# A mixture-of-experts kernel on one core: two blocks sorted together in the last step, running sums in reduced-precision products, and a new table of slots

## What is computed

```python
x = x + 0.5 * ffn0(layernorm(x))   # step 0
x = x + attn0(layernorm(x))
x = x + 0.5 * ffn0(layernorm(x))   # step 1
x = x + 0.5 * ffn1(layernorm(x))   # step 2
x = x + attn1(layernorm(x))
x = x + 0.5 * ffn1(layernorm(x))   # step 3
```

```python
kv = cumsum(einsum('bhtf,bhtg->bhtfg', K, V), axis=2)
Z = 1.0 / (einsum('bhtf,bhtf->bht', Q, cumsum(K, axis=2)) + 1e-06)
out = einsum('bhtf,bhtfg->bhtg', Q, kv) * Z[..., None]
```

## Time and profile before

| | us |
|---|---|
| median of 3 runs | 795.04 |
| lowest, highest | 790.27, 796.32 |
| the profiled execution, its own time | 787.4 |
| its span, first to last instruction | 785.7 |
| mean granted clock of TensorE, share of full speed | 0.929 |

### The profile page before, as it was taken

How to read it: one execution, slowest core, us unless ns; L and a number is a source line. 1 busy time by engine, 2 the same in 40 slices (tenths; PEclk the granted TensorE clock), 3 DMA queues, 4 the chain that set the end, 5 groups by cost and what they waited for, 6 DMA issues and landing times.

```text
span 785.7 us, 15361 instructions
## 1 busy us (share of the span) xinstructions
PE 631.2 (80%) x4586; PEld 571.3 (73%) x4586; DVE 392.2 (50%) x1357; ACT 255.5 (33%) x531; POOL 315.9 (40%) x352
## 2 busy tenths in 40 slices
PE   1298577969979796777888795999898988988975
PEld 1298466949768596677788794888787777887975
DVE  4373432725437163524354351775674855754165
ACT  1143332533415242323333241423423434232320
POOL 3545351271442516270716235225335354154314
PEclk9999897999999899887999798998999999989989
DMA  9378482735628266565767574665464554756942
GB/s 313 118 227 243 129 251 85 207 119 152 188 70 232 89 181 195 162 185 157 231 179 230 149 211 128 178 166 142 144 172 134 172 140 122 221 140 177 297 131 44
DMA packets 113796, 133.83 MB, mean 170 GB/s; under 512 B 10947, under 2 KB 76755, under 8 KB 113334
## 3 DMA queue, kind: packets, MB, share of 16 engines
q1 hardware_dynamic: 105526, 116.06, 51.0%
q0 software_dynamic: 8192, 16.79, 7.3%
HBM read 104.09 MB, written 28.71 MB: 169 GB/s over the span
## 4 chain that ended last, share of the span: by engine, by line
PE 58%; issue 19%; DVE 7%; another core or an unknown queue 5%; POOL 5%; ACT 4%; DMA 1%; SPq 1%; POOLq 0%; DVEq 0%; ACTq 0%
PE up_gate L983 16%; PE up_gate L976 13%; PE y L937 9%; PE side L991 3%; PE side L1057 2%; PE y L939 2%; PE side L1007 2%; PE side L1002 1%; POOL rows_dram L477 1%; DVE hidden L661 1%; ACT hidden L562 1%; PE side L1091 1%; POOL b_rstd L469 1%; PE side L1065 1%
## 5 line engine op out<-in xcount | busy, mean ns | idle before, releaser
L661 DVE TENSOR_TENSOR hidden<-up_gate,hidden 128x256 f32<-128x256 f32 (+1 forms) x240 | 116.0, 488 | 250.9 <-ACT hidden L562 84.0
L983 PE MATMUL up_gate<-rows_T,up 128*128 128x128 f32 x1440 | 199.2, 288 | 43.5 <-issue 21.7
L983 PEld LDWEIGHTS up_gate<-rows_T,up 128*128 128x128 f32 x1440 | 184.1, 202 | 57.0 <-issue 35.7
L562 ACT ACTIVATE hidden<-up_gate 128x256 f32<-128x256 f32 (+1 forms) x240 | 104.6, 436 | 322.4 <-PE up_gate L976 123.8
L477 POOL DMA_INDIRECT rows_dram<-rms_out,rows_of x128 | 128.2, 1002 | 176.9 <-DVE rows_of L801 142.4
L976 PE MATMUL up_gate<-rows_T,up 128*128 128x128 f32 x960 | 142.0, 295 | 18.4 <-ACT rows_T L567 6.6
L976 PEld LDWEIGHTS up_gate<-rows_T,up 128*128 128x128 f32 x960 | 128.5, 207 | 27.2 <-DVE hidden L661 13.2
L495 POOL DMA_INDIRECT y_rows<-y_dram,rows_of x120 | 122.1, 1018 | 56.6 <-issue 36.0
L937 PE MATMUL y<-down,hidden 128*128 x480 | 77.0, 285 | 4.8 <-issue 2.5
L937 PE MATMUL y<-down_a,hidden 128*128 x480 | 76.8, 285 | 0.0
L937 PEld LDWEIGHTS y<-down,hidden 128*128 128x128 f32 x480 | 66.6, 201 | 5.8 <-issue 5.8
(11 more groups left out here) (172 smaller groups left out, 671.8 us busy)
## 6 DMA issues: line engine op xcount, KB each, us to landing
up<-in_up SPq DMA_DIRECT2D x120, 352.0 KB
up<-in_up SPq DMA_DIRECT2D x120, 256.0 KB
rows<-rows_dram SPq DMA_DIRECT2D x48, 256.0 KB
y_dram<-y_tile SPq DMA_DIRECT2D x45, 256.0 KB
rows_dram<-zeros SPq DMA_DIRECT2D x12, 256.0 KB, 4.2
rows<-rows_dram SPq DMA_DIRECT2D x16, 192.0 KB
y_dram<-y_tile SPq DMA_DIRECT2D x15, 192.0 KB
rows_dram<-rms_out,rows_of POOLq DMA_INDIRECT x128
```

The costliest lines, as they stand in the source:

```text
L562: act.activation(hid[n % 4][:, 0:w], src, ACT.Silu).then_inc(silu_done, 1)
L661: dve.tensor_tensor(h, u, h, ALU.mult).then_inc(mult_done, 1)
L983: last = pe.matmul(U[q % 3][:, c * P:(c + 1) * P], upW[n % RING][:, at + c * P:at + (c + 1) * P], rows_, start=True, stop=True)
```

## The change

Group 4 = blocks 1 and 2 is new, and used in step 3 alone: 15 + 23 + 15 = 53 tiles there, so 233 slots in all. Block 1 still has 45 slots from its end to the group's start, block 2 has 30 and block 3 has 38. Block 2 therefore takes its own offsets (WAY = 1): attention 7 to 18, routing from 18, assign at 20, and scatter from 21, which now writes all 16 pieces of the group in the slots 186 to 193. The group's rows are loaded at slot 190 and transposed at 193, and its first tile is slot 195. LAG puts block 2's gathering 7 slots behind block 1's. Attention of the other blocks goes from offsets 14 to 31 to 8 to 22, with the following routing 9 slots earlier.

Each running-sum product becomes two: ACT copies k times v to fp32r (`kv_hi`), DVE subtracts that from the original (`kv_lo`), and PE multiplies both by fp32r ones. All other slots move too, among them LATE_MATRIX and the early store of the last group.

```diff
-GROUPS = [[0], [1], [2], [3]]
-STEP = [[0, 1, 2, 3], [0, 1, 2, 3], [0, 1, 2, 3], [0, 1, 2, 3]]
+GROUPS = [[0], [1], [2], [3], [1, 2]]
+STEP = [[0, 1, 2, 3], [0, 1, 2, 3], [0, 1, 2, 3], [0, 4, 3]]
...
-LAG = (1, 13, 9, 17, 9)
-
-COMBINE = (((8, 11),),
-           ((10, 13),),
-           ((7, 8),),
-           ((7, 9),))
-ATTENTION = (({3: 12, 4: 12, 5: 12, 6: 13, 7: 15, 8: 16, 9: 17, 10: 17, 11: 17, 12: 18, 13: 18, 14: 18, 15: 19},),
+LAG = (1, 24, 19, 32, 7)
+
+COMBINE = (((8, 10),),
+           ((8, 11),),
+           ((6, 6), (6, 6),),
+           ((7, 10),))
+ATTENTION = (({3: 11, 4: 11, 5: 11, 6: 12, 7: 14, 8: 15, 9: 16, 10: 17, 11: 18, 12: 19, 13: 19, 14: 19, 15: 20},),
              None,
-             ({3: 14, 4: 15, 5: 15, 6: 17, 7: 18, 8: 21, 9: 21, 10: 21, 11: 23, 12: 23, 13: 24, 14: 24, 15: 25, 16: 26, 17: 28, 18: 28, 19: 28, 20: 30, 21: 31},),
+             ({3: 8, 4: 8, 5: 8, 6: 8, 7: 10, 8: 11, 9: 11, 10: 11, 11: 12, 12: 12, 13: 15, 14: 15, 15: 16, 16: 17, 17: 18, 18: 19, 19: 19, 20: 21, 21: 22},
+              {3: 7, 4: 7, 5: 8, 6: 8, 7: 9, 8: 10, 9: 10, 10: 10, 11: 12, 12: 12, 13: 14, 14: 14, 15: 14, 16: 15, 17: 16, 18: 16, 19: 17, 20: 18, 21: 18},),
              None)
...
-         ({"stats": 31, "guess": 31, "root": 31, "norm": 31, "skip": 33, "z": 33, "score": 33, "first": 33, "second": 33, "rank": 35, "assign": 35, "weights": 36, "scatter": 37},))
-WAY = ((0, 0, 0, 0), (0, 0, 0, 0), (0, 0, 0, 0), (0, 0, 0, 0), (0, 0, 0, 0))
+         ({"stats": 22, "guess": 22, "root": 22, "norm": 22, "skip": 29, "z": 24, "score": 24, "first": 24, "second": 24, "rank": 26, "assign": 26, "weights": 27, "scatter": 28},
+          {"stats": 18, "guess": 18, "root": 18, "norm": 18, "skip": 24, "z": 19, "score": 19, "first": 19, "second": 19, "rank": 20, "assign": 20, "weights": 26, "scatter": 21},))
+WAY = ((0, 0, 0, 0), (0, 0, 0, 0), (0, 0, 0, 0), (0, 0, 1, 0), (0, 0, 0, 0))
...
-LATE_T, LATE_STORE, LATE_LOAD = (LATE_AT - LATE + at for at in (-7, 3, 5))
-LATE_MATRIX = [LATE_AT - LATE + at for at in (8, 9, 10, 11, 12, 13, 15)]
+LATE_T, LATE_STORE, LATE_LOAD = (LATE_AT - LATE + at for at in (-10, -9, -7))
+LATE_MATRIX = [LATE_AT - LATE + at for at in (-5, 2, 5, 6, 8, 9, 12)]
...
-                    if END_ROUND[r] + (STORE if (s, g) != LAST else 3) - 1 == t:
+                    if END_ROUND[r] + (STORE if (s, g) != LAST else 1) - 1 == t:
...
+                    if j in (13, 14, 15, 16):
+                        t = j - 13
+                        act.wait_ge(kv_ready, 4 * ka - 3 + t)
+                        act.activation(kv_hi[t][:, :], R[3 + t], ACT.Copy).then_inc(hi_ready, 1)
...
+                if l == 1 and j in (14, 15, 16, 17):
+                    t = j - 14
+                    dve.wait_ge(hi_ready, 4 * ka - 3 + t)
+                    dve.tensor_tensor(kv_lo[t][:, :], R[3 + t], kv_hi[t][:, :].bitcast(F32), ALU.subtract).then_inc(lo_ready, 1)
...
-                        pe.wait_ge(kv_ready, 4 * ka - 3 + t)
+                        pe.wait_ge(lo_ready, 4 * ka - 3 + t)
...
-                        last = pe.matmul(o, tri[:, :], R[3 + t], start=True, stop=(t % 2 == 0))
+                        pe.matmul(o, tri_r[:, :], kv_hi[t][:, :], start=True, stop=False)
+                        last = pe.matmul(o, tri_r[:, :], kv_lo[t][:, :], start=False, stop=(t % 2 == 0))
                         if t % 2:
-                            last = pe.matmul(o, ones[:, :], R[2 + t], start=False, stop=True)
+                            pe.matmul(o, ones_r[:, :], kv_hi[t - 1][:, :], start=False, stop=False)
+                            last = pe.matmul(o, ones_r[:, :], kv_lo[t - 1][:, :], start=False, stop=True)
```

More of the change, by code:

```diff
@@ L77 @@
              None)
-ROUTE = (({"stats": 2, "guess": 2, "root": 2, "norm": 3, "skip": 9, "z": 5, "score": 6, "first": 8, "second": 8, "rank": 10, "assign": 10, "weights": 11, "scatter": 16},),
-         ({"stats": 19, "guess": 19, "root": 20, "norm": 21, "skip": 23, "z": 23, "score": 24, "first": 25, "second": 27, "rank": 29, "assign": 29, "weights": 38, "scatter": 29},),
-         ({"stats": 15, "guess": 15, "root": 16, "norm": 20, "skip": 29, "z": 22, "score": 23, "first": 24, "second": 25, "rank": 27, "assign": 27, "weights": 36, "scatter": 29},),
-         ({"stats": 31, "guess": 31, "root": 31, "norm": 31, "skip": 33, "z": 33, "score": 33, "first": 33, "second": 33, "rank": 35, "assign": 35, "weights": 36, "scatter": 37},))
@@ L82 @@
-WAY = ((0, 0, 0, 0), (0, 0, 0, 0), (0, 0, 0, 0), (0, 0, 0, 0), (0, 0, 0, 0))
+ROUTE = (({"stats": 2, "guess": 2, "root": 2, "norm": 3, "skip": 10, "z": 4, "score": 6, "first": 7, "second": 7, "rank": 8, "assign": 8, "weights": 10, "scatter": 16},),
+         ({"stats": 20, "guess": 22, "root": 23, "norm": 23, "skip": 23, "z": 26, "score": 27, "first": 28, "second": 28, "rank": 30, "assign": 30, "weights": 30, "scatter": 30},),
+         ({"stats": 11, "guess": 12, "root": 14, "norm": 14, "skip": 16, "z": 15, "score": 16, "first": 16, "second": 17, "rank": 19, "assign": 19, "weights": 24, "scatter": 29},),
+         ({"stats": 22, "guess": 22, "root": 22, "norm": 22, "skip": 29, "z": 24, "score": 24, "first": 24, "second": 24, "rank": 26, "assign": 26, "weights": 27, "scatter": 28},
+          {"stats": 18, "guess": 18, "root": 18, "norm": 18, "skip": 24, "z": 19, "score": 19, "first": 19, "second": 19, "rank": 20, "assign": 20, "weights": 26, "scatter": 21},))
@@ L193, in macaron @@
         xT = sb("attn_xT", NT)
+        kv_hi = [sb(f"kv_hi{i}", NT, F32R) for i in range(TB)]
+        kv_lo = [sb(f"kv_lo{i}", NT, F32R) for i in range(TB)]
+        tri_r = sb("tri_r", P, F32R)
+        ones_r = sb("ones_r", P, F32R)
         spare = sb("spare", 2)
@@ L312, in macaron @@
         qkv_ready, min_ready, v_ready, exp_ready = sem("qkv_ready"), sem("min_ready"), sem("v_ready"), sem("exp_ready")
-        phi_ready, kv_ready, kcum_ready, den_used = sem("phi_ready"), sem("kv_ready"), sem("kcum_ready"), sem("den_used")
+        phi_ready, kv_ready, hi_ready, lo_ready, kcum_ready, den_used = sem("phi_ready"), sem("kv_ready"), sem("hi_ready"), sem("lo_ready"), sem("kcum_ready"), sem("den_used")
         cum_ready, cum_used = sem("cum_ready"), sem("cum_used")
@@ L641, in _ @@
             act.activation(spare[:, 0:1], ones[:, 0:1], ACT.Silu)
+            act.activation(tri_r[:, :], tri[:, :], ACT.Copy)
+            act.activation(ones_r[:, :], ones[:, :], ACT.Copy).then_inc(const_pe, 1)
             act.wait_ge(norm_loaded, 32)
@@ L1144, in _ @@
             pe.wait_ge(consts, 7)
-            pe.wait_ge(const_pe, 1)
+            pe.wait_ge(const_pe, 2)
             pe.wait_ge(norm_loaded, 32)
```

## The result

The changed kernel takes **819.11 us** (median of 4 runs, 816.34 to 828.08), the kernel before on the same chip 795.68 (790.27 to 799.23): the ratio is **1.032**, 95% interval 1.022 to 1.042. I had forecast 777.3. It is slower, and the range to 797 doesn't hold it.

What follows compares the result with a forecast made beforehand. PE was taken to set the pace, with stalls between. The terms -14.9 - 8.0 + 4.0 - 3.4 + 7.0 - 3.0 + 0.6 sum to -17.7 us, giving 777.3 on the median's base; whole range 757 to 797.

Steps and rivals of the forecast that it cites:

- The moved slots of layer 0 keep their number of operations and of bursts; I count 0.: Layer 0's moved slots: no change in time, with 4 us to either side of 337 us.
- "-8.0" for the sums: Running sums on PE: twelve one-pass fp32r products replace six fp32 ones a block, saving 8.0 us over four blocks.
- What the sums need in return, +4.0: ACT's copies and DVE's subtractions for the sums: ACT hides its part, DVE's costs 1 us a block, +4.0 us.
- Earlier attention, -3.4: Layer 1's attention: the sum of k moves to three slots behind phi, so its waits go, -3.4 us.
- The common group, +7.0: Blocks 2 and 3 before the group's tiles: waits for scattered rows, late normalising and lower clock, +7.0 us.
- "-14.9" for the tiles: Seven slots of layer 1 go, each 2.01 us on PE plus 0.11 for transposes: -14.9 us.
- The end, -3.0: Behind the last tile: gathers end sooner, -2.0, and DVE makes the matrices of weights earlier, -1.0; -3.0 us.
- "+0.6" for the start: Before slot 0: POOL's tables grow by 13 small fills of 0.04 each, +0.6 us.
- (b): Rival: gain given back by the group's unhidden wait, DVE's work in full and gather stalls; 796 us, chance 0.14.
- (c): Rival: POOL's products behind the previous block's scatters end each attention; 810.7 us by profile, 818 on median, chance 0.05.
- (d): Rival: in the running sums, fp32r is no faster than fp32 by instruction; 806 us, chance 0.05.

Runs made afterwards that it cites:

- e2: The kernel before with layer 0's new slots and nothing else: 664.70 us, ratio 1.023 to the kernel before.
- e5: The whole changed kernel again, on a chip where the kernel before takes about 651 us: 678.73 us, ratio 1.041.
- e1: The changed kernel with layer 0's slots (attention, combines, routing into steps 0 to 2) as before: 668.96 us, ratio 1.026 to the kernel before.
- e6: The kernel before with only step 0's routing in its new slots: 656.06 us, ratio 1.009.
- e3: The kernel before with only the sums as two fp32r products, with ACT's copies and DVE's subtractions: 654.76 us, ratio 1.007.
- e7: e3 without the subtraction, the second product taking the high half again: 641.68 us, ratio 0.984 to the kernel before.
- e8: The kernel before, fp32 sums and blocks sorted alone, with only the new slots between step 2 and step 3: 656.22 us, ratio 1.008.
- e4: The changed kernel with each block sorted alone, so without the common group: 675.22 us, ratio 1.038 to the kernel before.
- e15: The kernel before with fp32r sums of the high half alone, one product each, rerun on a slow chip: 795.57 us, ratio 0.987.
- e16: e2 again, on a slow chip: 821.15 us, ratio 1.023 to the kernel before.

## Why the prediction was wrong

The forecast of -17.7 us stands against +27.6 on B (678.73 less 651.14) and +23.4 on A. By its own steps, on B:

- **"The moved slots of layer 0 keep their number of operations and of bursts; I count 0."** This is the step that failed most: +14.2 us (e2, 664.70 against 650.48; 9.8 by e5 less e1), and 2.3% on D as well. Counting operations doesn't price a table of slots. What counts is the distance between the slot that issues a chain (DVE's statistics, POOL's power of 1.7, DVE's normalising of 1.3) and the slot in which PE, which runs up to one slot ahead, asks for its end. In step 0's routing, the part that e6 tests, one slot less made PE's wait 1.5 us longer in both blocks whose chain lies behind slot 0; for the other two thirds of the 14.2 the same is likely and not shown. Both conditions under which the prediction called itself wrong were met on A: layer 0 moved by over 5 us, and the steps of layer 1, which were to lose 10 us, became 3.8 longer (15.0 - 11.2).
- **"-8.0" for the sums** was right, and a little low: 9.5. The product's pace of 0.23 us lies near the low end that I had given it (0.215).
- **"What the sums need in return, +4.0"** was mis-sized: putting the subtraction back costs 13.1 us (e3 less e7), and PE's waits in front of the sums' products alone are 9.3 in e3's trace. I had summed DVE's load over five slots, at 0.69 a subtraction. I hadn't seen that it stands beside POOL's products (up to 3.28), nor that a third link pushes the denominator and the next tile's product behind it.
- **"Earlier attention, -3.4"** had the wrong sign: the new slots between step 2 and 3 cost 5.1 us (e8). I priced the one wait that they take away and none that they bring, above all the combine at offset 6 before the gathers have landed (PE stands 4.88 us in e8), and the normalising in the slot of POOL's power (2.95 at slot 159). In e5 the first of these is followed by the half clock, 1.4 us more. POOL's own chain went as I had drawn it: block 1's third product ends 6.2 us into slot 165, where I had 5.9; but the "0" behind it was wrong, since PE waits 2.9 us for the subtraction there.
- **"The common group, +7.0"** named the right wait and was half of what the group cost before its first tile: slots 165 to 195 are 15.3 us longer in e5 than in e4. The row numbers are there 3.0 us into slot 186 (I took 2), the 16 scatters and what stands between end 24.3 us in (23.8), SP's load goes out at 25.6, and PE stands 6.0 us where I had 7.5, less 3.6 as hidden. Of these 3.6, 1.7 were: PE asked 22.6 us into slot 186 and not 20.9. What I had left out is that block 2's attention and routing, squeezed between slots 172 and 184, have waits of their own (2.2, 0.9, 0.7 and 3.6 us at 179, 181, 183 and 184), and that the clock is lower through the whole stretch (0.90 against 0.93).
- **"-14.9" for the tiles** held, and was low: from slot 195 on 19.8 us go from e4 to e5, 17.6 of them PE's busy time. A slot takes 2.6 us there with what stands between, not the bare 2.01.
- **"The end, -3.0"** had the wrong sign: +2.7 on B (21.2 against 18.5), +4.0 on A. Without the group the new tables of the end bring 3.8 us (e4), near my 3.0; the group takes 6.5 back. I had the 12 gathers in turn, but let them end 7.9 us behind the last tile; it was 10.3, where it was 9.9 before by the earlier trace rows. Nearly all of the 2.4 is POOL's wait of 2.29 us in front of the first of them, at 652.89, for DVE's adding of other results to x.
- **"+0.6" for the start** was right for the constants (slot 0 begins 0.6 us later in e1, which has them and layer 0's old slots), but it is 2.4 in e5 and 2.0 in e6: with step 0's new slots PE stands 3.6 us in front of slot 0 for ACT's rows_T where it was 1.7, another part of layer 0's tables counted at nothing.

Added up, these sizes are -19.8 - 9.5 + 13.1 + 5.1 + 15.3 + 2.7 + 0.6 + 14.2 = 21.7. They come from medians, from single traces and from different kernels, and 5.9 of the 27.6 are placed by none of them.

Of the rivals, (b) named the right places (group unhidden, DVE's work in full, the stalls on the busiest slots) but took back only what was gained. (c), POOL's products behind the scatters of the block before as the end of each attention, was not the mechanism: scatters do stand between POOL's products in e5's block 1, but PE's waits for the sums' operand are 2.9 us at slot 166 and 2.2 at 179, not 10 in each block. (d) is refuted by the product's 0.23 us. That (c)'s price, 818, is next to the 819.11 measured is chance: its mechanism isn't what took the time. None of the rivals had layer 0.

## What to carry over

A change of a table of slots is a change of slack, and has to be priced link by link: for each value that PE asks for, the chain of other engines from its first instruction to its last, in us, against the slots between. Where a kernel is tuned so that PE stands almost nowhere (14 of 329 us in layer 1 on B), a chain that is made denser shows, and a stall can cost again in clock, as the one in front of slot 144 did. A faster matmul that needs one more elementwise link in front is worth the product's gain less that link's wait: here the products gave 9.5 us, ACT's copy took nothing of it, and the subtraction 13 on DVE and 19 on POOL.

## What the chip showed that I hadn't expected

- The same kernel takes 646 to 654 us on three chips, and 790 to 812 in the first comparison and on C and D. On B no wait of PE between slots 120 and 179 is over 1.1 us, and these slots take 156.76 us at a clock of 1.00; on A they take 198.4 at 0.92, with the same instructions. On A, in the burst of the earlier trace rows, ACT's next silu starts at 595.39 after 3.78 us of waiting, though the matmuls of its tile were issued at 589.85; the trace names no releaser:

```profile
595.39 0.49 ACT L562 ACTIVATE hidden<-up_gate 128x384 f32<-128x384 f32 x1 [3.78 <-remote]
```

  The chain that ended last gives "another core or an unknown queue" 16% of the span in the changed kernel on A, 13 and 15% in e15 and e16 on D, and nothing in e5 on B. I didn't find the cause, and tried nothing on it. It may be why layer 0 lost 21.5 us on A against 15.1 on B up to slot 120: attentions that moved into a burst would pay for it only there. That is argued from the two traces and not shown; on D, a slow chip too, layer 0's slots cost the same 2.3% as on B (e16).
- An fp32r product of 128 by 512 columns takes 0.23 us from start to start, little more than half of one of fp32's two instructions (0.43).
- A subtraction of 0.68 us takes 0.96 to 3.28 beside POOL's products, and never over 0.69 away from them (e3 to e5).
